# Numerators of a linear attention as full 128-column tiles, in another place of TensorE's order

## The reference

```python
q, k, v = (heads(Wq), heads(Wk), heads(Wv))        # 16 heads of 64
qp = _favor_plus(q, W_feat)                        # exp(q.W - |q|^2/2), 128 features
kp = _favor_plus(k, W_feat)
def step(carry, qkv):                              # over time, causal
    S = S + einsum('bhd,bhe->bhde', k_t, v_t)
    z = z + k_t
    num = einsum('bhd,bhde->bhe', q_t, S)
    den = einsum('bhd,bhd->bh', q_t, z) + EPS
    return ((S, z), num / den[..., None])
y = y.transpose(0, 2, 1, 3).reshape(Bb, Tt, H * HD)
return y @ Wo
```

## Time and profile before

| | before |
|---|---|
| median of 3 runs | 260.74 us |
| profiled execution, its own time | 261.14 us |
| its span | 259.3 us (1.8 us lie around it) |
| TensorE busy | 244.4 us (94%) |
| weight loads busy | 191.7 us (74%) |
| VectorE busy | 186.6 us (72%) |
| ScalarE, GpSimd busy | 146.4 us (56%), 101.5 us (39%) |
| mean granted TensorE clock | 0.979 |

### The profile page before, as it was taken

One profiled execution on the slowest core, in us unless ns is written; L12 is line 12 of the kernel. 1 busy time (PEld: TensorE's weight loads), 2 busy tenths in 40 slices (PEclk: granted clock), 3 DMA queues, 4 the chain that ended last, 5 costly groups with the idle time before them and its releaser, 6 DMA issues.

```text
span 259.3 us, 7034 instructions
## 1 busy us (share of the span) xinstructions
PE 244.4 (94%) x2746; PEld 191.7 (74%) x2752; DVE 186.6 (72%) x474; ACT 146.4 (56%) x284; POOL 101.5 (39%) x139
## 2 busy tenths in 40 slices
PE   7979999999999999999999999999969889999984
PEld 7844467786687678777777778787758778888853
DVE  3586688676833686777887897856556879998995
ACT  1333454454445887665776667666707157877772
POOL 2161113342302568335662688365500023434430
PEclk9979799999999999999999999999979999999999
DMA  6999999970079001100110000000000000010001
GB/s 210 374 382 402 396 399 370 379 278 3 1 223 335 10 0 47 40 3 4 40 43 3 4 3 0 3 3 4 3 0 3 3 1 3 0 43 20 21 25 61
DMA packets 15378, 26.83 MB, mean 103 GB/s; under 512 B 1233, under 2 KB 8689, under 8 KB 15345
## 3 DMA queue, kind: packets, MB, share of 16 engines
q1 hardware_dynamic: 14848, 26.28, 28.3%
q10 hardware_dynamic: 496, 0.10, 0.2%
HBM read 25.33 MB, written 1.05 MB: 102 GB/s over the span
## 4 chain that ended last, share of the span: by engine, by line
PE 66%; DVE 17%; issue 5%; POOL 5%; ACT 3%; DMA 2%; SPq 0%; DVEq 0%; POOLq 0%; ACTq 0%
PE b L1331 11%; PE b L1092 7%; PE b L1373 7%; PE b L1093 6%; PE b L1094 6%; PE b L1350 5%; PE b L1254 3%; PE b L1206 3%; PE b L1250 3%; PE b L1257 3%; PE b L1172 2%; DVE yT_lo L964 2%; PE b L1503 2%; DMA xwq<-in_xWq 2%; DVE smk L910 2%
## 5 line engine op out<-in xcount | busy, mean ns | idle before, releaser
L593 ACT ACTIVATE phi<-b 128x512 f32<-128x512 f32 x48 | 26.0, 598 | 15.3 <-PE b L1331 15.3
L842 DVE TENSOR_TENSOR x_lo<-b,x_hi 128x512 fp32r<-128x512 f32 x32 | 21.7, 688 | 16.8 <-ACT x_hi L460 16.7
L343 POOL TENSOR_TENSOR lnr<-lnv,mh 128x1 f32<-128x1 f32 x16 | 8.8, 552 | 60.8 <-DVE lnv L709 60.8
L400 POOL TENSOR_TENSOR sq_lo<-sq_sum,sq_hi 128x512 fp32r<-128x512 f32 x16 | 20.6, 1287 | 25.9 <-ACT sq_hi L460 25.9
L518 ACT ACTIVATE sq<-b 128x512 f32<-128x512 f32 x32 | 19.3, 603 | 18.2 <-PE b L1094 18.2
L394 POOL TENSOR_TENSOR sq_sum<-sq,sq 128x512 f32<-128x512 f32 x16 | 20.7, 1293 | 21.7 <-ACT sq L518 21.7
L1092 PE MATMUL b<-nT_lo,wp_hi 128*128 128x512 f32 x64 | 26.8, 419 | 0.1
L1373 PEld LDWEIGHTS b<-va,smk 128*64 128x64 f32 x512 | 18.3, 142 | 11.3 <-issue 7.2
L1373 PE MATMUL b<-va,smk 128*64 128x65 f32 x512 | 21.8, 232 | 5.0 <-DVE y L932 2.8
L1093 PE MATMUL b<-nT_hi,wp_lo 128*128 128x512 f32 x64 | 25.1, 391 | 0.0
L1094 PE MATMUL b<-nT_hi,wp_hi 128*128 128x512 f32 x64 | 25.0, 391 | 0.0
(11 more groups left out here) (178 smaller groups left out, 628.6 us busy)
## 6 DMA issues: line engine op xcount, KB each, us to landing
cT<-in_ctxT SPq DMA_DIRECT2D x8, 1028.0 KB, 12.0
cn<-in_ctx SPq DMA_DIRECT2D x8, 1024.0 KB, 10.6
wv_raw<-in_aWv SPq DMA_DIRECT2D x1, 1024.0 KB, 14.2
wp_raw<-in_aWq SPq DMA_DIRECT2D x4, 256.0 KB, 4.8
wp_raw<-in_aWk SPq DMA_DIRECT2D x4, 256.0 KB, 5.0
w_raw<-in_w2T SPq DMA_DIRECT2D x1, 1024.0 KB, 5.7
wo<-in_aWo SPq DMA_DIRECT2D x1, 1024.0 KB, 8.3
w_raw<-in_w1T SPq DMA_DIRECT2D x1, 1024.0 KB, 5.1
```

The costliest lines, as they stand in the source:

```text
L400: nc.gpsimd.tensor_tensor(sq_lo[n % 2][:], sq_sum[:], sq_hi[n % 2][:].bitcast(F32), ALU.subtract).then_inc(sq_l, 1)
L593: nc.scalar.activation(phi(n, a)[:], feature_bank(a), ACT.Exp).then_inc(f_exp, 1)
L842: nc.vector.tensor_tensor(x_lo[n % 2][r][:], proj_bank(n, r), x_hi[n % 2][r][:].bitcast(F32), ALU.subtract).then_inc(x_l, 1)
```

## The change

Each group of 128 tokens gets one numerator matmul with all 128 query columns as weights, instead of one for each half of 64: 4 matmuls in a call instead of 8. The rows of the product are the same, since `smk` has zeros in the cross blocks. In the order of TensorE, the numerators of the first head of a pair now stand behind the scores, and those of the second head behind the projection of the next step; DVE's order follows. Step 15 has scores 12, numerators 22, scores 13, numerators 23. The code behind the steps is unchanged but for the tile form.

```diff
--- before.py
+++ after.py
@@ -946,13 +946,14 @@
                 u = n - 3
+                if u >= 2:
+                    outputs(2 * u - 3)
+                if u >= 0:
+                    masked(u)
                 if u >= 1:
                     outputs(2 * u - 2)
-                if u >= 0:
-                    masked(u)
                 if n == STEPS - 1:
                     masked(u + 1)
-                if u >= 1:
                     outputs(2 * u - 1)
@@ -1369,24 +1370,24 @@
                 for g in range(HALF):
-                    for b in range(P // PT):
-                        mm = pe.matmul(value_bank(v)[PT * b:PT * (b + 1), g * VW:(g + 1) * VW],
-                                       smk[u % 2][:, a * HALF + g, b, :], va[:, HALF * h + g, head, :],
-                                       start=True, stop=True)
+                    mm = pe.matmul(value_bank(v)[:, g * VW:(g + 1) * VW],
+                                   smk[u % 2][:, a * HALF + g].rearrange("p b n -> p (b n)"),
+                                   va[:, HALF * h + g, head, :], start=True, stop=True)
                 mm.then_inc(n_mm, 1)
 
             def slot(n):
                 u = n - 3
+                attention(u)
                 if u >= 1:
                     numerators(2 * u - 2)
-                attention(u)
                 if n == STEPS - 1:
                     attention(u + 1)
-                if u >= 1:
                     numerators(2 * u - 1)
 
             for n in range(1, STEPS):
                 project(n, 0, 1)
+                if n >= 5:
+                    numerators(2 * (n - 4) - 1)
```

## The result

| | before | after |
|---|---|---|
| median of the runs beside each other | 260.41 us | 273.16 us |
| profiled execution, its span | 261.14, 259.3 us | 270.58, 268.8 us |
| TensorE, weight loads busy | 244.4, 191.7 us | 254.5, 206.0 us |
| VectorE busy | 186.6 us | 186.0 us |

The ratio is 1.041, 95% interval 1.031 to 1.052. The four runs after took 270.58, 270.40, 275.75 (mean granted clock 0.963) and 1363.87 us; the last two were slow ones, so the ratio leaves them out and the profiled 270.58 us, not the median, stands for the kernel. I forecast +5.6 us, 266.7, range 261.5 to 270. The profiled execution is +9.4, just outside.

The account below looks back on a forecast made before the run. TensorE's own time was taken to bound the kernel. Terms 4.4 - 0.5 + 1.1 - 0.7 + 0.6 + 0.0 + 0.7 gave +5.6 us on the profiled 261.14, so 266.7 us, range 261.5 to 270.

Parts of the forecast that it names:

- The cost of a full tile: Numerator calls: a full-tile pass costs its weight load, 0.111 us, so a call takes 0.89 us instead of 0.51.
- The first load hidden behind a projection: Numerators behind a projection: the first load hides under 512 moved columns, leaving 7 x 0.111 = 0.78 us.
- the three changes of form: Each step: three changes between tile forms as before, about 0.10 us each.
- the wait for y gone with nothing in its place: Steps 5 to 14: the 0.21 us wait of second numerators for y of the first goes; none replaces it.
- the terms of step 4, of numerators 26, 28 and 30: Step 4: -0.5 us; numerators 26 and 27: +0.6; 28 and 29, under a wait: +0; 30 and 31: +0.7.
- The rivals with shorter or longer passes: Full-tile passes: 0.095 us gives 263.3 (chance 0.2); 0.057, load hidden, 256.0 (0.08); 0.166, load plus movement, 278 (0.03).
- the ten steps: Steps 5 to 14: 7.77 us each against 7.33, +4.4 us in all.
- passes of 256 columns would need over 0.3 if load and movement added up: Argument from 256-column passes, at most 0.255 us each, that a pass costs its load, not load plus movement.
- the bound of 0.057 for 65 columns: Lower bound in us for a full-tile numerator pass if its load hides; that rival gave 256.0, chance 0.08.
- mask 13 to 7.8, y of 23 to 8.65. Numerators 24 start 0.15 later, at 8.8: +1.1.: Step 15, from the projection's end: DVE's masks and y set the start of numerators 24, +1.1 us.
- One of 1.24 us left the clock at 1.00; I take it that it stays.: Before numerators 24: a 1.4 us wait keeps the clock up; the rival, a fallen clock, gave 268.5, chance 0.2.
- the 0.7 gain: Numerators 24 to numerators 26: 3.94 us instead of 4.67 with the clock staying up, -0.7 us.

Follow-up runs that it names:

- The third buffer: Changed kernel with mask 13 writing a buffer of masked scores of its own, so it no longer waits for numerators 23; median 269.6 us, ratio 1.027.
- filling the wait: Changed kernel with 11 matmuls of 512 columns, results unread, in the 2.5 us wait before numerators 24; median 269.9 us, ratio 1.033.
- tile-only: Kernel before with full-tile numerators in their old places; median 273.2 us, ratio 1.053.

## Why the prediction was wrong

**Right.** The cost of a full tile: 0.111 taken from loads under 2-column matmuls, 0.115 measured. The Trainium skill, "TensorE: Matmul & The Clock Gate", section "LDWEIGHTS (loading the stationary operand)", has the load time follow the weight columns alone, columns over 1.2 in ns, 107 for 128; the trace agrees in kind if that is read as the distance from load to load, which is 8% above, while a single load is recorded as 200 ns long. The first load hidden behind a projection, the three changes of form, the wait for y gone with nothing in its place, the terms of step 4, of numerators 26, 28 and 30: each within 0.1 us. The rivals with shorter or longer passes fell. Direction and cause of the slowing in the steps were right; the ten steps cost 5.1 and not 4.4, since each call took 0.02 to 0.04 more than its term. Two of the arguments for that cost were weaker than they read. That passes of 256 columns would need over 0.3 if load and movement added up comes from no row: a projection moves 512 columns in 0.23, and half of that with a load of 0.111 is 0.23, which the 0.255 at most of the earlier trace rows allows. What ruled the sum out is the run with 33 columns. And no row gives the bound of 0.057 for 65 columns; the rows give 0.065 at most.

**Wrong, first step: "mask 13 to 7.8, y of 23 to 8.65. Numerators 24 start 0.15 later, at 8.8: +1.1."** It let mask 13 start when y of 22 was done, and took DVE's own work for the bound. Line 907 makes mask u wait for numerators of pair u - 2, and for u = 13 the second of these, numerators 23, now stands behind scores 13, a change of form and y of 22. In the steps this wait is met long before; only in step 15, with two masks in one step, is it the last. In the trace before, numerators 23 end at 187.98:

```profile
187.34 0.64 PE L1373 MATMUL b<-va,smk 128*64 128x65 f32 x16
```

DVE ends mask 12 at about 188.07, half of the 2.88 us from 186.63. So the condition was met just as DVE was free, the row named nobody, and I took the engine for the bound. In the changed kernel numerators 23 end at 194.13 and mask 13 starts at 194.24, where I had it start 1.4 us earlier. The third buffer showed it: 1.4 us.

**Wrong, second step: "One of 1.24 us left the clock at 1.00; I take it that it stays."** It fell in the changed kernel and behind 1.10 us as well. I had given this 0.2 and a price of 1.8 us; filling the wait showed 2.75, since in this trace 5.8 us of work stand at the low clock where I counted numerators 24 and 25 alone (3.6). Against the 0.7 gain that I had booked, the stretch came out 2.7 off, the largest part of the miss.

Together 1.4 + 2.7 + 0.7 in the steps, less 1.0 at the start, is 3.8, the distance from +5.6 to +9.4. The 1.0 at the start is luck: without it the miss would have been 4.8. The range reached 270 with the fallen clock at 1.8 us on top of passes of 0.118 (268.2), and no case had the later mask.

## What to carry to other kernels

In this kernel two half-width fp32 tiles beside each other took 0.064 us a pair of passes, one full tile 0.115 with 65 or with 33 moved columns. So before merging tiles that move few columns, price the loads: half the instructions went here, and TensorE became slower. Look for what ends a wait in the code, not in the row: when two conditions are met together the trace names one, and a change can move the other. Where TensorE is the bound, look for work that is due anyway to put into a wait of 1 to 3 us: here the last exponents took 4.1 us off that stretch in the kernel before and 5.0 in the changed one.

## What was not expected of the hardware

The clock stood at 1.2 GHz for 16.2 us while TensorE was busy throughout, in the profiled execution of the kernel with 33 moved columns; in the changed kernel it was 5.8 us of work, in tile-only and in the kernel before about 3.4. Mean clocks between 0.956 and 0.981 in four executions of the first suggest that the length varies from execution to execution. The same kernels kept 1.00 in the steps, with the same numerators among projections. The fall does not come at a fixed distance from the wait either: of two waits of 2.53 us, one saw it 1.6 us after it began (changed kernel), the other 3.8 us after, when TensorE was at work again (tile-only). And idle times of 1.24 us (clock kept) and 1.10 us (clock lost) show that length alone does not decide; what else does is open.
